# Feed-forward prologue of a decoder layer: two weights turned through four banks, the third inside the first row group

## The reference: what is computed

```python
w1, w2, w3 = (nf4_roundtrip(w) for w in (weight1, weight2, weight3))
# w1, w2: 1408 x 512; w3: 512 x 1408, bf16 levels times block scales
x = x + (silu(LN(x) @ w1.T) * (LN(x) @ w2.T)) @ w3.T
```

## Time and profile before

| | us |
|---|---|
| Median of 3 runs | 2444.95 (2437.4 to 2446.93) |
| The profiled execution | 2442.58 |
| its span | 2440.8 |
| PE busy | 2211.7 (91%) |
| DVE, ACT, POOL busy | 1612.8, 776.0, 756.5 |
| mean granted TensorE clock | 0.932 of 2.4 GHz |

### The profile page before, as it was taken

The page is one execution under the profiler, slowest core; times in us unless marked ns, Lnnn a source line. Parts: engine busy times, 40 slices in busy tenths (PEclk is TensorE's granted clock), DMA queues, the critical chain, the costliest instruction groups (busy, mean ns, idle before and its releaser), DMA issues. The chain is left out here.

```text
span 2440.8 us, 35529 instructions
## 1 busy us (share of the span) xinstructions
PE 2211.7 (91%) x11766; PEld 1577.0 (65%) x11766; DVE 1612.8 (66%) x2879; ACT 776.0 (32%) x1804; POOL 756.5 (31%) x531
## 2 busy tenths in 40 slices
PE   6899999999999999999999973788988897679998
PEld 4778888888877888888888861333333332257777
DVE  6668788888866568878887733567777777442221
ACT  1213323222332332232223120154454555532221
POOL 3324433433442443453353322111112221111222
PEclk9899999999999999999999986688788998869999
DMA  5211101101111201110110006825565554301100
GB/s 186 84 38 50 49 13 55 50 15 47 49 50 62 70 15 42 49 55 6 55 49 18 3 18 150 137 82 102 117 127 124 120 107 90 101 35 52 52 35 18
DMA packets 58085, 157.21 MB, mean 64 GB/s; under 512 B 9510, under 2 KB 24302, under 8 KB 51446
## 3 DMA queue, kind: packets, MB, share of 16 engines
q1 hardware_dynamic: 56742, 153.55, 23.7%
q10 hardware_dynamic: 1248, 2.46, 0.6%
HBM read 113.25 MB, written 34.33 MB: 60 GB/s over the span
## 5 line engine op out<-in xcount | busy, mean ns | idle before, releaser
L1501 DVE TENSOR_REDUCE x_mx<-x_pm 128x1 f32<-128x512 f32 x512 | 316.1, 679 | 76.5 <-PE x_pm L1598 75.3
L1334 ACT ACTIVATE x_E<-x_pd 128x512 f32<-128x512 f32 x512 | 265.5, 603 | 226.6 <-PE x_pd L1612 225.6
L1598 PE MATMUL x_pm<-x_K,x_Q 53*128 53x512 f32 x512 | 191.2, 514 | 44.7 <-DMA x_K<-parts_scratch 24.7
L659 DVE TENSOR_TENSOR a_rm<-a_pj,a_rope 128x1024 f32<-128x1024 f32 x128 | 155.8, 1218 | 113.0 <-PE a_pj L930 111.4
L1612 PE MATMUL x_pd<-x_Q,x_K 54*128 54x512 f32 x512 | 180.5, 514 | 49.8 <-DMA x_Q<-maxima_scratch 25.0
L1612 PEld LDWEIGHTS x_pd<-x_Q,x_K 54*128 54x128 f32 x512 | 76.9, 203 | 225.3 <-ACT x_E L1334 116.2
L442 ACT ACTIVATE a_v<-a_pj 128x256 f32<-128x256 f32 x128 | 49.1, 384 | 414.6 <-PE a_pj L946 414.6
L568 POOL TENSOR_TENSOR a_ogl<-a_ogf,a_ogh 128x512 fp32r<-128x512 f32 x64 | 81.3, 1291 | 292.7 <-ACT a_ogf L473 292.7
L1626 PE MATMUL x_pa<-x_E,x_vx 128*32 128x512 f32 x1024 | 153.4, 675 | 0.0
L930 PE MATMUL a_pj<-a_xh,a_wqk_h 128*128 128x512 f32 x512 | 150.8, 416 | 1.3 <-POOL a_wqk_l L538 1.3
L946 PE MATMUL a_pj<-a_wvg_h,a_xh 128*128 128x512 f32 x512 | 151.0, 417 | 1.0 <-DVE a_rm L659 1.0
(11 more groups left out here) (209 smaller groups left out, 4919.4 us busy)
## 6 DMA issues: line engine op xcount, KB each, us to landing
a_qk_raw<-in_wqk SPq DMA_DIRECT2D x16, 1024.0 KB, 5.4
a_vg_raw<-in_wvg SPq DMA_DIRECT2D x16, 1024.0 KB, 4.9
x_Q<-parts_scratch SPq DMA_DIRECT2D x42, 256.0 KB
x_K<-parts_scratch SPq DMA_DIRECT2D x42, 256.0 KB
a_wo_raw<-in_wo SPq DMA_DIRECT2D x16, 512.0 KB, 3.6
parts_scratch<-x_hi SPq DMA_DIRECT2D x16, 512.0 KB, 2.8
parts_scratch<-x_lo SPq DMA_DIRECT2D x16, 512.0 KB, 3.3
a_acc<-in_w SPq DMA_DIRECT2D x6, 704.0 KB, 4.5
```

Source lines behind the costliest of these rows:

```text
L659: nc.vector.tensor_tensor(turned, pb, table, ALU.mult).then_inc(roped_m, 1)
L1334: nc.scalar.activation(E[:, n % ESLOTS, :], pd[:, n % 3, :], ACT.Exp, scale=XD ** -0.5).then_inc(exp_done, 1)
L1501: nc.vector.reduce_max(mx[:, u % 2, at:at + 1], pm[:, k % 3, :], AX_X).then_inc(pm_done, 1)
L1598: mm(pm[:, k % 3, :], Q[b % 3][z, hp, q * P:(q + 1) * P], K[b % 3][z, hp, :], start=True, stop=True).then_inc(pm_ready, 1)
```

## The change

The prologue turns only the first two weights, round by round, 11 rounds `r` of one tile each. The first weight's tiles go through the two banks `pa`, the second's through the two banks `pb`. ACT takes all of the first weight; DVE takes the second weight's first seven tiles (`BY_DVE = 7`), ACT its last four. DVE takes five tiles, then does the statistics, then two more tiles, then normalizes. From round 8 on (`MIXED = FT - 3`) PE turns one row tile after each round. The rows are loaded in two transfers, the first with a semaphore of its own. The f32 identity is loaded from ACT's queue, and PE waits for it at round 8 only.

The third weight is turned in the first row group: after each round's matmuls PE turns one tile into a `po` bank, and ACT copies it after `hh` of the round before. PE waits for all eleven before it goes on from the first stage of that group. Four semaphores are added.

```diff
--- before.py
+++ after.py
@@ -1672,34 +1672,39 @@
         sil, hf = sb("sil", [P, 2, 512]), sb("hf", [P, 2, 512])
         hh, hl = sb("hh", [P, FT, 512], F32R), sb("hl", [P, FT, 512], F32R)
         pa, pb, po, pt = banks("pa", 2), banks("pb", 2), banks("po", 2), banks("pt", 2)
-        (const_in, w_ready, taken_act, taken_dve, filled, x_in, r_in, stat, aggr, eps_done, rstd_done, xn_done,
+        (const_in, ident_done, w12_ready, taken_act, taken_dve, w3_ready, w3_taken, filled, x_first, x_in, r_in, stat, aggr, eps_done, rstd_done, xn_done,
          t_ready, xh_done, xl_done, a_ready, b_ready, sil_done, hf_done, hh_done, hl_done,
          y_ready, y_done, stored, carried) = s.sems(
-            "const_in w_ready taken_act taken_dve filled x_in r_in stat aggr eps_done rstd_done xn_done "
+            "const_in ident_done w12_ready taken_act taken_dve w3_ready w3_taken filled x_first x_in r_in stat aggr eps_done rstd_done xn_done "
             "t_ready xh_done xl_done a_ready b_ready sil_done hf_done hh_done hl_done "
             "y_ready y_done stored carried")
-        taken = (taken_act, taken_dve)
         block = s.enter_context(nc.Block())
-
-        TILES = []
-        for i, w in enumerate((w1, w2)):
-            for r in range(FT):
-                TILES.append((i, [(slice(r * D + c * P, r * D + (c + 1) * P)) for c in range(C)],
-                              w[:, :, r * P:(r + 1) * P]))
-        for r in range(FT):
-            TILES.append((2, [slice(q * FF + r, q * FF + r + (P - 1) * FT + 1, FT) for q in range(4)],
-                          w3[:, r, :].rearrange("p (d q) -> p q d", q=4)))
+        BY_DVE = 7
+        MIXED = FT - 3
+
+        def turned(i, r):
+
+            return pa[:, r % 2, 0:256].bitcast(BF16) if i == 0 else pb[:, r % 2, 0:256].bitcast(BF16)
+
+        def by_act(i, r):
+
+            return r + 1 + max(0, r + i - BY_DVE)
+
+        def spread(bank):
+
+            return bank.rearrange("p (q n) -> p q n", q=4)
 
         @block.sync
         def _(sp):
             sp.dma_start(identb[:], identb_in).then_inc(const_in, 16)
-            sp.dma_start(ident[:], ident_in).then_inc(const_in, 16)
 
             def load_x(g):
                 after(sp, xn_done, 4 * g)
                 sp.dma_start(xt[:], x2_in[bass.ds(g, 1)].rearrange("g t p d -> p (g t) d")).then_inc(x_in, 16)
 
-            load_x(0)
+            first = x2_in[0].rearrange("t p d -> p t d")
+            sp.dma_start(xt[:, 0:2], first[:, 0:2]).then_inc(x_first, 16)
+            sp.dma_start(xt[:, 2:4], first[:, 2:4]).then_inc(x_in, 16)
 
             def step(g, more):
                 if more:
@@ -1745,11 +1750,16 @@
 
         @block.scalar
         def _(act):
-            for t, (i, cols, dst) in enumerate(TILES):
-                if t % 2 == 0:
-                    act.wait_ge(w_ready, t + 1)
-                    src = pa[:, t % 2, 0:256].bitcast(BF16)
-                    nc.scalar.activation(dst, src.rearrange("p (q n) -> p q n", q=4), ACT.Copy).then_inc(taken_act, 1)
+            act.dma_start(ident[:], ident_in).then_inc(ident_done, 16)
+
+            def take(i, r):
+                act.wait_ge(w12_ready, 2 * r + i + 1)
+                nc.scalar.activation((w1, w2)[i][:, :, r * P:(r + 1) * P], spread(turned(i, r)), ACT.Copy).then_inc(taken_act, 1)
+
+            def take_w3(r):
+                act.wait_ge(w3_ready, r + 1)
+                nc.scalar.activation(w3[:, r, :].rearrange("p (d q) -> p q d", q=4), spread(po[:, r % 2, 0:256].bitcast(BF16)),
+                                     ACT.Copy).then_inc(w3_taken, 1)
 
             def high(g, tt):
                 act.wait_ge(t_ready, 4 * g + tt + 1)
@@ -1771,12 +1781,19 @@
                         act.wait_ge(hf_done, n + 1)
                         after(act, y_ready, 4 * g)
                         nc.scalar.activation(hh[:, f - 1, :], hf[:, (f - 1) % 2, :], ACT.Copy).then_inc(hh_done, 1)
+                        if isinstance(g, int) and g == 0:
+                            take_w3(f - 1)
                 if more:
                     for tt in range(4):
                         high(g + 1, tt)
 
-            for tt in range(4):
-                high(0, tt)
+            for r in range(FT):
+                take(0, r)
+                if r >= BY_DVE:
+                    take(1, r)
+                if r >= MIXED:
+                    high(0, r - MIXED)
+            high(0, 3)
             step(0, True)
             with act.Fori(1, G - 1) as g:
                 step(g, True)
@@ -1787,9 +1804,15 @@
             V = nc.vector
 
             def norm_stats(g):
-                dve.wait_ge(x_in, 16 * g + 16)
-                after(dve, rstd_done, g)
+                first = isinstance(g, int) and g == 0
+                if first:
+                    dve.wait_ge(x_first, 16)
+                else:
+                    dve.wait_ge(x_in, 16 * g + 16)
+                    dve.wait_ge(rstd_done, g)
                 for tt in range(4):
+                    if first and tt == 2:
+                        dve.wait_ge(x_in, 16)
                     V.bn_stats(stats[:, tt, :], xt[:, tt, :]).then_inc(stat, 1)
                 dve.wait_ge(stat, 4 * g + 4)
 
@@ -1845,20 +1868,23 @@
                 for tt in range(1, 4):
                     add(g, tt)
 
+            def take(r):
+                dve.wait_ge(w12_ready, 2 * r + 2)
+                V.tensor_copy(w2[:, :, r * P:(r + 1) * P], spread(turned(1, r))).then_inc(taken_dve, 1)
+
+            for r in range(BY_DVE - 2):
+                take(r)
             norm_stats(0)
+            for r in range(BY_DVE - 2, BY_DVE):
+                take(r)
             normed(0, 0)
             normed(0, 1)
-            for t, (i, cols, dst) in enumerate(TILES):
-                if t % 2 == 1:
-                    dve.wait_ge(w_ready, t + 1)
-                    src = pa[:, t % 2, 0:256].bitcast(BF16)
-                    V.tensor_copy(dst, src.rearrange("p (q n) -> p q n", q=4)).then_inc(taken_dve, 1)
-            for pair in range(2):
-                if pair:
-                    normed(0, 2)
-                    normed(0, 3)
-                for tt in (2 * pair, 2 * pair + 1):
-                    low(0, tt)
+            low(0, 0)
+            normed(0, 2)
+            low(0, 1)
+            normed(0, 3)
+            low(0, 2)
+            low(0, 3)
             step(0, True)
             with dve.Fori(1, G - 1) as g:
                 step(g, True)
@@ -1867,7 +1893,7 @@
         @block.tensor
         def _(pe):
             mm = nc.tensor.matmul
-            pe.wait_ge(const_in, 32)
+            pe.wait_ge(const_in, 16)
 
             def transpose_x(g, tt):
                 pe.wait_ge(xn_done, 4 * g + tt + 1)
@@ -1879,15 +1905,33 @@
                     last = nc.tensor.transpose(pt[:, tt % 2, c * P:(c + 1) * P], xn[:, tt % 2, c * P:(c + 1) * P], ident[:])
                 last.then_inc(t_ready, 1)
 
-            for t, (i, cols, dst) in enumerate(TILES):
-                after(pe, taken[t % 2], t // 2)
-                for q, col in enumerate(cols):
-                    last = nc.tensor.transpose(pa[:, t % 2, q * 64:(q + 1) * 64].bitcast(BF16), raw[:, i, col], identb[:])
-                last.then_inc(w_ready, 1)
-            for tt in range(4):
-                transpose_x(0, tt)
-            pe.wait_ge(taken_act, (len(TILES) + 1) // 2)
-            pe.wait_ge(taken_dve, len(TILES) // 2)
+            def turn(i, r):
+                if r >= 2 and i and r - 2 < BY_DVE:
+                    pe.wait_ge(taken_dve, r - 1)
+                elif r >= 2:
+                    pe.wait_ge(taken_act, by_act(i, r - 2))
+                for c in range(C):
+                    last = nc.tensor.transpose(turned(i, r)[:, c * P:(c + 1) * P], raw[:, i, r * D + c * P:r * D + (c + 1) * P], identb[:])
+                last.then_inc(w12_ready, 1)
+
+            def turn_w3(r):
+                if r >= 2:
+                    pe.wait_ge(w3_taken, r - 1)
+                for q in range(4):
+                    last = nc.tensor.transpose(po[:, r % 2, q * 64:(q + 1) * 64].bitcast(BF16),
+                                               raw[:, 2, q * FF + r:q * FF + r + (P - 1) * FT + 1:FT], identb[:])
+                last.then_inc(w3_ready, 1)
+
+            for r in range(FT):
+                turn(0, r)
+                turn(1, r)
+                if r == MIXED:
+                    pe.wait_ge(ident_done, 16)
+                if r >= MIXED:
+                    transpose_x(0, r - MIXED)
+            transpose_x(0, 3)
+            pe.wait_ge(taken_act, 2 * FT - BY_DVE)
+            pe.wait_ge(taken_dve, BY_DVE)
 
             def step(g, more):
                 pe.wait_ge(xl_done, 4 * g + 4)
@@ -1903,6 +1947,10 @@
                                 last = mm(bank[:, f % 2, :], w[:, c, f * P:(f + 1) * P], x[:, c, :],
                                           start=k + c == 0, stop=k * C + c == 2 * C - 1)
                         last.then_inc(ready, 1)
```

(4 more changed lines are left out.)

## The result

| | before | changed |
|---|---|---|
| median of 15 runs, us | 2444.95 | 2423.13 |
| lowest and highest | 2435.47, 2458.24 | 2419.12, 2439.88 |
| profiled execution, its span | 2442.58, 2440.8 | 2419.12, 2417.3 |
| mean granted clock | 0.932 | 0.94 |

The ratio of the changed kernel to the one before is 0.9924, with a 95% interval of 0.9904 to 0.9944; in microseconds that is 18.6, with an interval of 13.7 to 23.5. Timed again later the ratio was 0.9889 (0.9865 to 0.9912). The medians lie 21.8 us apart; the forecast was 2426.4, 18.5 less.

A forecast was written before the change was run, and what follows sets the result against it. About 40 us of weight preparation before the feed-forward part, with no engine full, was taken to bound the kernel. 22.3 - 2.7 - 0.8 - 0.3 = 18.5 us less, so 2426.4 us against the median of 2444.95; range 2418 to 2434.

The forecast's parts named there:

- The prologue: Weight preparation before the feed-forward part: first matmul 17.8 us after PE's first transposition, 22.3 us less than before.
- about 16.8: Prologue bound: if PE's clock doubled halfway, the chain of readers would still hold it to about 16.8 us, gaining 23.3.
- I took 1.2 GHz for the whole prologue: Prologue: TensorE's clock stays at 1.2 GHz throughout, although PE is denser in it than before.
- rival 1: Dense prologue raises the clock: 1.0 us there and 2.0 in the first 16 matmuls, so 2423.4 us; chance 0.15.
- The reason I gave: Kernel before, prologue: 14 us with PE busy 10.3 in transpositions left the clock at 0.50; later matmuls raised it.
- The third weight: First row group: 44 transpositions on PE's path at 0.06 us each, 2.7 us more.
- the bounds of 2.3 and 4.5: Third weight's transpositions in the first row group: 2.3 us at 0.052 each, 4.5 us all at low clock.
- ACT's copies at nothing: First row group: ACT's 11 copies of 1.09 us fit its 2.51 us idle before each silu, costing nothing.
- The end of the group: First row group's end: PE waits for ACT's eleventh copy before turning rows; 0.7 or 1.4 us more, taken as 0.8.
- The split of the load: Prologue: loading the rows in two parts gives nothing; it is cover of 0.9 us for a late landing.
- The semaphores: Kernel's end: four more semaphores cleared by POOL, 0.3 us more; 25 took 1.6 us.
- The slower rival: First row group: transpositions breaking up matmuls drop the clock, up to 37.9 us more, 2464.4 us; chance 0.04.

The follow-up runs named there:

- the extra transpositions: Changed kernel plus 32 unread identity transpositions while PE waits for DVE's sixth tile and 16 while it waits for the last xl: 2413.3 us.
- one load: Changed kernel with the rows loaded in one transfer instead of two: 2419.91 us.
- later wait: Changed kernel with PE's wait for the eleventh third-weight copy moved behind turning the next group's two row tiles: 2426.09 us.
- changed kernel again: The changed kernel as it is, timed again beside the kernel with extra transpositions and the wait moved: 2421.01 us, ratio to before 0.9889.
- one bank a weight: Changed kernel with the first two weights' tiles through one bank each, two in all instead of four: 2429.77 us.
- all three together: Changed kernel with one bank for each of the first two weights, DVE's statistics ahead of its tiles, and row tiles last: 2435.63 us.
- the filled version: Changed kernel plus unread transpositions in two idle prologue pieces and the third-weight wait moved later, timed twice: 2421.34 and 2419.16 us, ratios 0.9896 and 0.9908.

## Why the prediction was right, point by point

*The prologue.* Forecast: first matmul 17.8 us behind PE's first transposition. Measured 16.3 (2130.87 to 2147.20). DVE's fifth tile, the statistics, PE's one stand behind DVE's sixth tile (3.03 for 2.7) and the waits of the last row tile all came in the forecast order. Along the forecast's own chain, DVE began the statistics 4.6 behind the first transposition instead of 5.2, since its tiles no longer came 0.86 apart; PE was on again at 8.4 instead of 9.1; the last row tile began at 14.2 instead of 15.15; and its tail was 2.16 instead of 2.62.

All but 0.1 of that stands in pieces where the clock was full for part of the time. The profiles of this prologue bear it out: from the first transposition to the first matmul it is 16.3 where the clock rose some 3 us behind the start (two profiles), 16.7 where it rose 5 us behind it (three), and 15.8 to 16.0 with the extra transpositions (three). The prediction had worked this out as the bound "about 16.8". So the step "I took 1.2 GHz for the whole prologue" failed, and rival 1's first half came true. Its second half (the first 16 matmuls at full clock) didn't in this profile, 5.59 us as before, but did in three of the five profiles with this prologue and no extra transpositions (4.0: one load, later wait, changed kernel again). The rival had been given 0.15; its 2423.4 lies nearer to the median of 2423.13 than the forecast does, though its sum has the same small term for the third weight.

The reason I gave, that 14 us of transpositions had left the clock low, read the wrong cause out of the row: PE had gaps of 0.36 in every pair there. The three kernels with one bank a reader (before, one bank a weight, all three together) have the gaps, and the clock stays low as long as tiles run in pairs; in all eleven profiles with four banks it rose inside the prologue; and useless transpositions in PE's stand hold it. The Trainium skill, "TensorE: Matmul & The Clock Gate", PE-mode transpose, says that the full clock doesn't engage for transpose mode, which doesn't count as being busy; these runs contradict it (1.00 from 2133.8 in the changed kernel, with nothing but transpositions before), and the measurement decides.

*The third weight.* Forecast 2.7 us, measured about 4.1 (11 x 0.37). The transposition was right at 0.055 for 0.06; the 0.15 a round that stands beside the transpositions was missing. I had counted only the added instructions. The measured term stayed inside the bounds of 2.3 and 4.5. By the Trainium skill, "TensorE: Matmul & The Clock Gate", Back-to-back issue gap, 81 ns for a pair of weight load and matmul would have given 3.6. That is nearer to the total, but not as a pair's price: that is 0.055 here.

*ACT's copies at nothing.* Right: ACT still has 1.88 us to spare before each silu. I had 1.4 left; the round is longer by 0.37.

*The end of the group.* Forecast 0.7, or 1.4 if the clock had already fallen when the rows run, taken as 0.8. Measured between the same stamps: 0.5 (3.42 for 2.94) in three profiles where it hadn't fallen and 1.1 (4.05) in the profiled one, where it had. Both cases came as named, each 0.2 to 0.3 smaller. Since this span begins with the eleventh tile, that tile is in it already, and ten tiles, 3.7 us, are what the third weight adds beside it.

*The split of the load.* Nothing, as forecast, in this order. In the order of before the statistics came 1.8 earlier (4.41 for 6.20), and how much of that is the split wasn't tried.

*The semaphores.* 2.0 us from PE's drain to POOL's, for 1.6: 0.4 for 0.3.

```profile
L107 PEldq DRAIN  x1: 13/13/13, 2415.1 to 2415.1; - x1
L107 POOLq DRAIN  x1: 41/41/41, 2417.1 to 2417.1; - x1
```

*The sum.* By the measured terms of this profile: 23.7 + 0.05 - 3.3 - 1.2 - 0.4, 18.8 us that the change made, against 18.5. That agreement is luck, two misses that cancel: the prologue gave 1.4 that I had not counted, by the clock, and the first group's first stage with its end took 4.5 instead of 3.5. In the second profile of the changed kernel the same sum is 20.0, as its first matmuls ran at full clock. The other 3.0 of the 21.8 between the medians weren't traced, since only single executions are profiled, and the interval takes them in. In the profiled pair, 4.6 us more than the 18.8 went, into the clock at the group ends (3.4) and an earlier block start (1.2). The block's start differs by 9.5 us between the two profiles of the changed kernel. The ends of the later groups differ between kernels whose code is the same there, so I don't count them for the change; in the two profiles of the changed kernel they were alike.

*The slower rival* asked whether transpositions inside the group bring the low clock. From 2151 to 2192.5 PE was busy for 41.5 us of 41.5 at 1.00: they don't. In all twelve profiles with the third weight in the group the clock, once up, stayed up to the last round.

## What to carry to other kernels

Where one engine fills a bank and another empties it, two banks a reader turn the sum of their times into the larger of the two, and with TensorE as the filler the missing gaps may also bring its clock up; then the readers set the pace. Price all three. Work put into a full engine costs its own instructions and something for each visit (0.15 us here), so put it there in few, larger pieces. Before you credit an edit with a microsecond, look at the clock in both profiles: 0.6 of the later wait's 1.0 was that. And undo the parts one at a time before naming what brought the gain: three parts here were worth 4.2, 1.5 and 0.9 us alone, 9.1 together.

## What the runs showed of the hardware

Transpositions raise and hold TensorE's clock: dense ones raised it some 3 us after they began in the changed kernel (2130.87 to 2133.8), and 3.1 to 5.2 us after in nine other profiles. It fell again at 2140.7, 4.4 us after an idle piece had begun at 2136.3, when PE was already at work again. Where tiles ran in pairs with gaps of 0.16 to 0.36 us between them it stayed low, for 8.5 us in the run with one bank a weight and for 22 us in the kernel before.

A visit of bf16 transpositions between f32 matmuls costs about 0.15 us at full clock, beside 0.055 for each transposition. Which part of the visit costs it is open.

At the ends of the later groups, where all these kernels have the same code, some profiles kept the full clock and others lost it, at 1.7 or 3.4 us each time. The two profiles of the changed kernel agree in this, and so do the two of the filled version. A change that shifts everything behind it by some microseconds may gain or lose that much there, as the filled version did.
